# A router before a mixture-of-experts layer: logits the other way round, fewer table steps, later weight requests

## The reference, cut to what matters

```
tokens = layernorm(x).reshape(-1, 256)                 # 4096 tokens
probs  = softmax(tokens @ Wr + br)                     # 8 experts
expert = argmax(probs);  max_prob = probs[expert]
h   = relu(tokens @ W1[expert] + b1[expert])           # 256 -> 512
out = h @ W2[expert] + b2[expert]                      # 512 -> 256
x   = x + out * max_prob
```

## Time and profile before

| | us |
|---|---|
| median of 3 runs | 1510.41 |
| the profiled execution | 1510.09 |
| its span | 1508.1 |
| PE busy (x6834 matmuls) | 1358.1 (90%) |
| DVE / ACT / POOL busy | 1042.3 / 959.1 / 850.9 |
| chain that ended last | PE 63%, ACT 14%, DVE 13%, issue 8% |

### The profile page before, as it was taken

How to read it: one execution, slowest core, us unless ns; L and a number is a source line. 1 busy time by engine, 2 the same in 40 slices (tenths; PEclk the granted TensorE clock), 3 DMA queues, 4 the chain that set the end, 5 groups by cost and what they waited for, 6 DMA issues and landing times.

```text
span 1508.1 us, 21846 instructions
## 1 busy us (share of the span) xinstructions
PE 1358.1 (90%) x6834; PEld 922.1 (61%) x6834; DVE 1042.3 (69%) x1567; ACT 959.1 (64%) x1781; POOL 850.9 (56%) x413
## 2 busy tenths in 40 slices
PE   5999889999988988989989989999899878759997
PEld 2566645999744555555655655555556545449996
DVE  6666534333333898998899989998998998853332
ACT  1222231344325999898998998999989999104442
POOL 1111002555200898887888888878878889224552
PEclk9999999999988999999999999999999899979999
DMA  9200024676420697996996998979969989447662
GB/s 302 74 28 28 28 84 146 207 205 209 129 67 16 136 225 161 203 221 160 209 222 154 211 208 173 218 171 204 213 149 210 219 206 229 127 152 209 211 207 81
DMA packets 100116, 249.28 MB, mean 165 GB/s; under 512 B 10857, under 2 KB 41710, under 8 KB 85808
## 3 DMA queue, kind: packets, MB, share of 16 engines
q0 software_dynamic: 23248, 132.93, 40.6%
q1 hardware_dynamic: 74688, 113.62, 25.2%
q10 hardware_dynamic: 2080, 1.47, 0.3%
HBM read 116.65 MB, written 18.88 MB: 90 GB/s over the span
## 4 chain that ended last, share of the span: by engine, by line
PE 63%; ACT 14%; DVE 13%; issue 8%; DMA 1%; POOL 0%; DVEq 0%; POOLq 0%; ACTq 0%
PE ps L1515 11%; PE ps L1254 10%; PE ps L1455 9%; PE ps L1464 9%; ACT arena L698 5%; DVE arena L1152 5%; ACT arena L708 5%; PE ps L1546 4%; PE ps L1279 4%; PE ps L1316 2%; PE ps L1373 2%; PE ps L1270 2%; PE ps L1590 2%; PE ps L1411 1%; DVE x L1152 1%
## 5 line engine op out<-in xcount | busy, mean ns | idle before, releaser
L463 POOL TENSOR_TENSOR arena<-arena 128x2048 f32<-128x2048 f32 x97 | 446.4, 4602 | 149.7 <-DVE arena L1152 140.5
L1152 DVE TENSOR_TENSOR_SCAN arena<-arena,ps 128x512 f32<-128x512 f32 x392 | 471.4, 1212 | 60.6 <-PE ps L1254 52.2
L1254 PEld LDWEIGHTS ps<-cst,arena 128*128 128x128 f32 x2428 | 301.6, 145 | 322.4 <-issue 207.0
L1254 PE MATMUL ps<-cst,arena 128*128 128x128 f32 x2428 | 374.4, 282 | 79.0 <-ACT arena L708 39.2
L698 ACT ACTIVATE arena<-arena,a_neg 128x512 f32<-128x512 f32 x512 | 366.3, 715 | 46.1 <-DVE arena L1152 35.0
L708 ACT ACTIVATE arena<-arena,m_bt 128x512 f32<-128x512 f32 x512 | 363.2, 710 | 3.3 <-DVE arena L1083 2.2
L1515 PE MATMUL ps<-arena,tapw 128*128 128x512 f32 x512 | 260.5, 609 | 0.0
L432 POOL DMA_INDIRECT arena<-rows,arena x78 | 75.7, 970 | 176.9 <-DVE arena L1008 153.7
L1028 DVE TENSOR_TENSOR arena<-ps,arena 128x256 f32<-128x256 f32 x78 | 33.2, 426 | 202.9 <-PE ps L1464 120.3
L1152 DVE TENSOR_TENSOR_SCAN x<-arena,ps 128x512 f32<-128x512 f32 x120 | 143.9, 1211 | 19.9 <-PE ps L1254 17.0
L1455 PEld LDWEIGHTS ps<-arena 128*128 128x128 f32 x1248 | 153.5, 194 | 3.8
(11 more groups left out here) (168 smaller groups left out, 1552.3 us busy)
## 6 DMA issues: line engine op xcount, KB each, us to landing
arena<-arena POOLq DMA_DIRECT2D x52, 1024.0 KB, 8.3
arena<-in_W SPq DMA_DIRECT2D x94, 512.0 KB, 7.9
x<-arena POOLq DMA_DIRECT2D x33, 1024.0 KB, 8.3
arena<-c_rows SPq DMA_DIRECT2D x128, 256.0 KB, 3.7
arena<-x POOLq DMA_DIRECT2D x16, 1024.0 KB, 8.8
rows<-x SPq DMA_DIRECT2D x16, 512.0 KB, 3.4
x<-x POOLq DMA_DIRECT2D x8, 1024.0 KB, 9.1
x<-residual SPq DMA_DIRECT2D x12, 512.0 KB, 5.5
```

Source lines behind the costliest of these rows:

```text
L463: g.tensor_tensor(h, h, m_c[i % RC].unsqueeze(1).to_broadcast([P, KI, SEQ]), ALU.mult)\
L1152: v.tensor_tensor_scan(out=h[:, k, :], data0=m_a[g % RA], data1=ps[SCAN_BANK[g % 3]][:, :], initial=0.0, op0=ALU.mult, op1=ALU.add).then_i ...
L1254: return t.transpose(bank, src[:, k * P:(k + 1) * P], ident)
```

## The change

- `logits` takes the tokens as stationary operand (128 x 128) and the 8 router columns as moving, two matmuls per chunk and eight per batch, and writes 128 x 32 directly. `lg_copy` and `lg_turn` are gone. In round 0 `x_turn(0, 1)` comes ahead of `logits(0, 0)`.
- Rows in DRAM have 258 values: 256 of x, mean and rstd. ACT writes those two (`scales_out`): two DMAs of 8 bytes per token, in round 0 behind `raw_copy` of batch 5, in round 1 ahead of the exponential. The gathers wait for them. `r_val` has two values (token, max_prob) instead of four; `norm` reads mean and rstd from the gathered row.
- The counting matmuls change places: `ones` first, with its own semaphore step, then `tri`. DVE starts on the totals when `ones` is done. Rounding uses one constant of 2^30 size, so a tile number costs one step instead of three. 12 linked or unlinked steps are left of the 17.
- W1 of tile 1 and all later ones is asked for only when the first gather has landed.
- Taps: (0,0) goes ahead of the counting matmuls, (0,1) and (1,0) behind them, (1,1) behind the last group, and the last four behind the expert loop. The last conv load moves behind all W1 requests of round 0 on SP.

```
-FEED_PAIR = ([((0, 4), (5, 1), (2, 3))[i % 3] for i in range(BATCH)], ...
+FEED_PAIR = ([((0, 4), (5, 2), (1, 3))[i % 3] for i in range(BATCH)], ...
-ROUND = 1.5 * 2 ** 23
-V_TOK, V_PMAX, V_MEAN, V_RSTD, NV = 0, 1, 2, 3, 4
+CEIL = 1.5 * 2 ** 30
+V_TOK, V_PMAX, NV = 0, 1, 2
+ROW = D + 2
+RUN = NCH + 1
...
 # SP, send_w1 (the wait), and the taps' loads
                 for j in range(TILES):
+                    if j == 1:
+                        sp.wait_ge(S("f_x0"), 16 * (r * ((TILES + XB - 1) // XB) + 1))
...
+            for k in range(TAPS - 1):
+                send_tap(k)
             send_w1(0)
+            send_tap(TAPS - 1)
 # POOL, send_tiles
                 g.wait_ge(S(f"f{r}_rows"), 16 * BATCH)
+                g.wait_ge(S("scales_out"), 32 * (r + 1))
 # ACT
-            def lg_copy(r, i):
...
+            def scales_out(r):
+                half = RING * SEQ
+                a.wait_ge(S("f_scales"), r + 1)
+                for i in range(2):
+                    lo = half * (i ^ r)
+                    a.dma_start(xs[r][lo:lo + half, D:ROW].rearrange("(c p) v -> p c v", p=P),
+                                scales[:, i * NCH // 2:(i + 1) * NCH // 2, :]).then_inc(S("scales_out"), 16)
...
             def feed(r):
+                if r:
+                    scales_out(r)
 # DVE, feed
-                v.wait_ge(S("by_ones"), 2 * r + 2)
-                link(v.tensor_copy(tot, ps[6][:, 0:NCH * E].rearrange("p (c e) -> p e c", e=E)))
...
+                v.wait_ge(S("by_ones"), 3 * r + 2)
+                link(v.tensor_reduce(r_tl, total[:, :, 1:RUN], AX.X, ALU.add))
+                link(v.tensor_scalar(r_tl, r_tl, 0.5 * (P - 1), CEIL, ALU.add, ALU.add))
+                link(v.tensor_scalar(r_tl, r_tl, -CEIL, None, ALU.add))
                 link(v.tensor_tensor_scan(out=r_te, data0=ones[:, 0:E], data1=r_tl, initial=0.0,
                                           op0=ALU.mult, op1=ALU.add))
...
+                v.tensor_scalar(r_tc, r_te, CEIL, None, ALU.add)
+                link(v.scalar_tensor_tensor(out=total[:, :, 0], in0=r_te, scalar=-1.0, in1=r_tl, op0=ALU.add,
+                                            op1=ALU.subtract))
+                link(v.tensor_tensor_scan(out=r_cum, data0=cst[:, C_RST:C_RST + E * RUN], data1=ps[6][:, 0:E * RUN],
+                                          initial=0.0, op0=ALU.mult, op1=ALU.add))
+                v.wait_ge(S("by_ones"), 3 * r + 3)
+                link(v.tensor_tensor(pm, rank, cum[:, :, 0:NCH], ALU.add))
                 link(v.tensor_tensor(pm, pm, oh, ALU.mult))
+                link(v.tensor_reduce(r_pf, r_pm.rearrange("p (e c) -> p c e", e=E), AX.X, ALU.add))
...
+                link(v.tensor_scalar(r_hi, r_pf, -0.5 * (P - 1), CEIL, ALU.add, ALU.add))
+                v.scalar_tensor_tensor(out=r_pf, in0=r_hi, scalar=-CEIL, in1=r_pf, op0=ALU.add, op1=ALU.subtract)\
                     .then_inc(S("f_place"), 1)
 # PE
             def logits(r, i):
...
+                for c in range(CPB):
+                    for k in range(KD):
+                        last = t.matmul(ps[FEED_PAIR[r][i][0]][:, c * E:(c + 1) * E], x_turned[r][i][:, k, c * P:(c + 1) * P],
+                                        wr[:, k, :], start=(k == 0), stop=(k == KD - 1))
...
             x_turn(0, 0)
+            x_turn(0, 1)
             logits(0, 0)
-            lg_turn(0, 0)
+            t.wait_ge(S("f_xt"), 2)
             a_oturn(BATCH - 1, BATCH - 1)
-            x_turn(0, 1)
+            logits(0, 1)
             a_out(BATCH - 1)
...
             def feed(r):
+                if r == 0:
+                    t.wait_ge(S("f_raw"), BATCH - 1)
+                    tap(0, 0)
                 t.wait_ge(S("f_lg"), 2 * r + 2)
-                t.matmul(ps[5][:, 0:NCH * E], tri, r_oh, start=True, stop=True)
-                t.matmul(ps[6][:, 0:NCH * E], ones, r_oh, start=True, stop=True).then_inc(S("by_ones"), 1)
+                t.matmul(ps[6][:, 0:E * RUN].rearrange("p (e c) -> p e c", e=E)[:, :, 1:RUN], ones,
+                         r_oh.rearrange("p (e c) -> p e c", e=E), start=True, stop=True).then_inc(S("by_ones"), 1)
+                t.matmul(ps[5][:, 0:NCH * E], tri, r_oh, start=True, stop=True).then_inc(S("by_ones"), 1)
                 if r == 0:
-                    for n in range(3):
+                    for n in range(1, 3):
                         tap(n // KD, n % KD)
...
-                    if r == 0 and i == 0:
-                        tap(1, 1)
                 if r == 0:
-                    for d in range(KD):
-                        tap(2, d)
-                    t.wait_ge(S("tapw"), KD * 3)
+                    tap(1, 1)
+                    t.wait_ge(S("tapw"), KD * 2)
...
             feed(0)
-            for d in range(KD):
-                tap(TAPS - 1, d)
+            for n in range(4, KD * TAPS):
+                tap(n // KD, n % KD)
```

More of the change, by code:

```diff
@@ L95 @@
 FEED_ORDER = (tuple(range(BATCH)), (4, 5, 0, 1, 2, 3, 6, 7))
-FEED_PAIR = ([((0, 4), (5, 1), (2, 3))[i % 3] for i in range(BATCH)], [(0, 1)] * 6 + [(2, 3), (0, 1)])
+FEED_PAIR = ([((0, 4), (5, 2), (1, 3))[i % 3] for i in range(BATCH)], [(0, 1)] * 6 + [(2, 3), (0, 1)])
 FEED_AT = (2, 10, 18, 26, 34, 42)
@@ L128 @@
 C_RST = 4 * P
-C_THR = C_RST + E * NCH
-C_DESC = C_THR + NCH
+C_DESC = C_RST + E * RUN
 C_IOTA = C_DESC + E
@@ L153, in build @@
         vals = sb("vals", [P, NCH, NV])
-        mean, rstd, pmax = [vals[:, :, i] for i in (V_MEAN, V_RSTD, V_PMAX)]
+        scales = sb("scales", [P, NCH, 2])
+        mean, rstd, pmax = scales[:, :, 0], scales[:, :, 1], vals[:, :, V_PMAX]
         cst = sb("cst", [P, C_ALL])
@@ L240, in build @@
         s = Space(tail)
-        t_x = [s.take(D) for _ in range(XB)]
+        t_x = [s.take(ROW) for _ in range(XB)]
         t_n = [s.take(D) for _ in range(2)]
         t_xt = [s.take(KD * P).rearrange("p (k t) -> p k t", k=KD) for _ in range(2)]
-        assert s.at <= router + 4 * NCH * E, s.at
+        assert s.at <= router + 5 * NCH * E, s.at
         s = Space(AR - 2 * KI * DI - KI * D - 3 * HID)
@@ L274, in build @@
         x_turned = ([f_xt[i % 2] for i in range(BATCH)], [halves[i // IN_LAST][i % 2] for i in range(BATCH)])
-        lg_turned = ([f_flat[i % 2][0:E, 0:SEQ] for i in range(BATCH)],
-                     [late[i // IN_LAST][0:E, (i % 2) * SEQ:(i % 2 + 1) * SEQ] for i in range(BATCH)])
         lg_raw = (r_pm, m_bc[:, 0:NCH * E])
@@ L280, in build @@
         ps = [ctx.enter_context(nc.psum_tensor(f"ps{i}", [P, 512], F32)) for i in range(8)]
-        xs = [nc.dram_tensor(f"rows{r}", (TOK + 1, D), F32, kind="Internal").ap() for r in range(2)]
+        xs = [nc.dram_tensor(f"rows{r}", (TOK + 1, ROW), F32, kind="Internal").ap() for r in range(2)]
         c_rows = [nc.dram_tensor(f"c_rows{i}", (NS, SEQ), F32, kind="Internal").ap() for i in range(2)]
@@ L355, in _, with send_tap @@
             sp.dma_start(ipw, T["ip_x"].rearrange("(k p) d -> p k d", p=P)).then_inc(S("ld_cw0"), 16)
-            for k in range(TAPS):
+            def send_tap(k):
                 if k >= 2:
@@ L577, in _, with tap_copy @@
                         x_copy(0, i, k)
[L578 to L588 removed]
+                if i - 1 >= 2:
+                    raw_copy(0, i - 1)
+                if i == BATCH - 2:
+                    scales_out(0)
+            def tap_copy(n):
+                a.wait_ge(S("tap_mm"), n + 1)
+                a.activation(tapw[:, n // KD, n % KD, :], ps[n % 2][:, :], ACT.Copy).then_inc(S("tapw"), 1)
             def feed(r):
+                if r:
+                    scales_out(r)
                 a.wait_ge(S("f_lg"), 2 * r + 1)
@@ L593, in feed @@
                 if r == 0:
-                    for k in range(TAPS // 2):
-                        tap_copy(k)
+                    for n in range(3):
+                        tap_copy(n)
                     a.wait_ge(S("ld_m"), 16 * 9)
@@ L775, in _ @@
                     x_copy(1, i, k)
-                lg_copy(1, i)
                 raw_copy(1, i)
@@ L809, in layer_norm_scales @@
                 link(v.tensor_scalar(y.bitcast(I32), d.bitcast(I32), -0.5, 1597463007.0, ALU.mult, ALU.add))
-                for _ in range(3):
+                for i in range(3):
                     link(v.tensor_tensor(q, y, y, ALU.mult))
                     link(v.scalar_tensor_tensor(out=t, in0=q, scalar=-0.5, in1=d, op0=ALU.mult, op1=ALU.mult))
-                    link(v.scalar_tensor_tensor(out=y, in0=t, scalar=1.5, in1=y, op0=ALU.add, op1=ALU.mult))
+                    last = v.scalar_tensor_tensor(out=y, in0=t, scalar=1.5, in1=y, op0=ALU.add, op1=ALU.mult)
+                    if i == 2 and done:
+                        last.then_inc(S("f_scales"), 1)
+                        v.wait_ge(S("f_scales"), done)
+                    else:
+                        link(last)
             def ln_apply(out, c):
```

115 lines of the change are left out of this document (35 added, 80 removed).

## The result

The changed kernel takes **1502.09 us** (median of 19 runs, 1496.16 to 1510.02) against 1510.88 (median of 19, 1509.01 to 1514.68): ratio **0.9947, 95% interval 0.9936 to 0.9958**. It is faster, by 0.5% instead of the predicted 2.2%; 1477 us was missed by 25 us and the range (1469 to 1493) too. The runs of the new kernel spread over 14 us, those of the old one over 6. The profiled execution took 1499.49 us (span 1497.7; before: 1508.1).

What follows compares the result with a forecast made beforehand. The prediction took a chain of waits between engines in both routers as the bound. Savings of 21.6 (round 0), -0.5 (behind the loop), 1.2 (last mamba batch) and 10.7 (round 1) sum to 33.0: from 1510.09 to 1477 us, range 1469 to 1493.

Steps and rivals of the forecast that it cites:

- Logits, 7.7: Round 0's router logits: copy, turn back and copy go; six batches save 6.0, first and last 1.7, in all 7.7 us.
- the logits matmuls are therefore not cheaper: Round 0's logits: sixteen 8-column records per batch at 0.11 to 0.13 each take 1.8 to 2.1 us, against 1.83 before.
- rival B: Logits: eight moving columns leave PE nearly empty, clock halves from batch 2, 16 us lost, total 1493; chance 0.12.
- ScalarE's two issues, 0: Issue of the mean and rstd writes on ACT, 0.59 each (1.2 for two), taken to fit into slack and cost nothing.
- Totals and places, 2.8 in round 0: Between logits and groups: `ones` first with PE warm saves 1.3, fewer DVE steps for places save 1.5 us.
- Groups, 7.8 and 3.4: Four one-hot groups up to `idx`: shorter groups, fewer taps ahead in round 0; 7.8 us saved there, 3.4 in round 1.
- Gather to first tile, 3.3 and 4.0: From `idx` to first tile: gather lands 2.6 after its start, stretch falls to 6.0; saves 3.3 and 4.0 us by round.
- rival A: First tiles: the wait moves from the gather to late W1 weights, 4 us in each round, total 1485; chance 0.12.
- the term of zero: W1 of tile 1, asked for later: needed 4.1 us after its request, first in its queue, so no wait was priced.
- Rival C: The 8-byte writes hold the gathers: nothing at 30 ns each, 1488 at 81 ns; chances 0.06 without loss, 0.03 slower.
- Behind the loop, -0.5: After round 0's expert loop: four taps instead of two delay ACT's normalising; 0.5 us lost, bounds -0.5 to +1.7 lost.
- The last mamba batch, +1.2: Last mamba batch before round 1: six `lg_copy` leave ACT's chain; 1.2 us saved, bounds 0 to 2.8.

Runs made afterwards that it cites:

- combo2: Changed kernel with 128-column logits, 160-column one-hot products, six unread matmuls in round 1 and the scales' writes on SyncE: 1483.0 us.
- scales_sp: Changed kernel with the two writes of mean and rstd issued by SyncE instead of ScalarE: 1499.18 us, ratio 0.9930 to the kernel before.
- wide kernels: Variants of the changed kernel whose logits matmuls move the same 8 columns 16 times (128 columns); with that edit alone 1492.98 us, ratio 0.9884.
- wide_grp: Changed kernel with each one-hot product moving its 80 columns twice (160 columns): 1495.34 us, ratio 0.9902 to the kernel before.
- warm_grp: Changed kernel with 160-column one-hot products and, in round 1, six unread 512-column matmuls behind the two sums: 1494.11 us, ratio 0.9884.
- pitch: Changed kernel with 128-column logits and DRAM rows 1088 bytes apart instead of 1032, padding zeroed by two extra DMAs: 1510.29 us, ratio 0.9993.
- mixed: Changed kernel with 128-column logits in round 0 and the old kernel's logits in round 1: 1495.59 us, ratio 0.9903 to the kernel before.
- combo4: combo2 plus the edits of pitch and gate2; total slower than the expected 1475 to 1478 us, its own time not given in the text.
- combo6: combo2 with five unread matmuls instead of six and round 1's logits in the old form; slower than 1478 to 1480 us expected, last batch 75.1 us.
- gate2: Changed kernel with 128-column logits and W1's third and fourth slots asked for behind the first relu: 1499.19 us, ratio 0.9923.
- again: The changed kernel without any edit, profiled a second time: 1505.26 us, ratio 0.9947 to the kernel before.

## Why the prediction was wrong, step by step

The step that failed is one premise in two places: that PE does narrow products at full clock. It failed in round 0's logits and in round 1's groups.

**Logits, 7.7: the step that failed.** At full clock the term is right: copy, turn back and copy did go, and they were worth 7.84 (`combo2`), where the clock stays and ScalarE has no issue in its way, and a narrow batch took 2.61 against the forecast 2.7. The step "the logits matmuls are therefore not cheaper" priced sixteen records at full clock, and the clock did not stay: 3.2 in the first profile, a loss of 3.5 to 4.8 in four others, 6.1 in `scales_sp`. This was rival B, given 0.12. Its arithmetic doubled turn and logits from the third batch on, 16 us; measured are 4.6 to 12.5 above the forecast stretch in five profiles and 1.6 in `scales_sp`. So its term was too large, and its 1493 is too low all the same, since it kept all the other terms at full clock. I had set it aside by the earlier trace rows, where PE, 0.85 of 3.00 us busy with transposes alone, kept 1.00. That row shows a short stretch of light work at full clock; what had to be priced was 20 us of turns and 8-column products without a gap. No row of before showed that, so both ends should have stayed open. The same trace even had a row for the other side, in round 1's logits, behind some 15 us of turns with pauses between them (the same four records took 1.88 at full clock; mean clock 0.57 from 1225 to 1230):

```profile
1225.16 3.58 PE L1373 MATMUL ps<-arena,wr 128*8 128x512 f32 x4 [0.22 <-ACT arena L547]
```

The Trainium skill ("TensorE: Matmul & The Clock Gate", Part 4) says that transposes don't count as PE-busy the same way; the runs agree so far that turns with narrow products go cold and the same turns with wide products do not. PE's busy share says nothing here: it was 12.00 of 12.00 us at 0.50.

**ScalarE's two issues, 0: mis-sized.** 1.2 by the earlier trace rows, a row from the start, and taken as hidden; they took 2.57 and 5.44. In round 0 they cost 0.9 to 2.1 where the clock holds (wide kernels). In round 1 they turn 2.4 (totals and places) into 0.6; `scales_sp` gives 2.2 there.

**Totals and places, 2.8 in round 0: right at full clock,** 2.75; 2.0 in the first profile, with a tap that began cold (5.23 instead of 3.5).

**Groups, 7.8 and 3.4: the clock again.** Round 0 gave 6.4; the last group's 3.28 us cold is the rest, and where it is warm it is 7.7. Round 1 gave nothing (-0.2). The sum had "PE cold at first"; that it would then warm up, as in the kernel before, was assumed, and that kernel's products were twice as wide. `wide_grp` and `warm_grp` show it (14.4 and 12.4 instead of 16.5).

**Gather to first tile, 3.3 and 4.0: right in the main,** 2.4 and 3.7, and 3.4 where the tap beneath it is warm. In the changed kernel's own two profiles PE never waits for W1 of tile 1. In five variants it does, by 0.7 to 1.3 us in round 0 (`warm_grp` 1.13, `pitch` 1.27, `mixed` 1.19, `combo4` 0.70, `combo6` 0.93), and for the third tile's by 2.49 in `gate2`. So rival A, 4 per round, did not come, but the term of zero has little to spare. Not in the sum at all was the relu behind it: 2.3 us from first to second layer, and 1.5 more for the cold layer that follows.

**Rival C is false as told.** POOL never waits for the writes. Queue 10 went from 0.3% to 0.6% with 8256 packets more: 0.3% x 16 x 1498 / 8256 is about 9 ns each, its lower end. (Its break-even is also a little off: 256 writes of 130 ns are 33.3 us, 8.3 over the 25 of round 0 and 24.3 over the 9 left in round 1, 32.6 in all.) The writes cost at their issue instead.

**Behind the loop, -0.5: right** (-0.7, 8.7 to 8.0).

**The last mamba batch, +1.2: -3.2.** 1.5 goes with the narrow logits in the stretch ahead of it: from output product to output product 103.0 instead of 101.5, in all six narrow profiles (102.9 to 103.0), and 101.5 to 101.8 in all others. The other 1.7 are open. In the first profile DVE's wait for broadcasts is 2.6 longer, but in `again` it is 1.5 and POOL's 3.8, as in the kernel before, and the batch takes 72.1 all the same. The size changes with each kernel (70.1 to 78.2 us for a batch of 70.2 before), and neither pitch nor the logits' form explains it alone. This batch is also where `combo2` loses 6 of the 17 us that it had gained by then.

Put together for the profile: start -1.0 (the last attends lie that far apart, the execution's doing: those of the old kernel's own two profiles lie 2.9 apart), logits 3.2, totals and places 2.0, groups 6.4, gather 2.4, relu -2.3, cold first turns and loop -2.0, behind it -0.7, last batch -3.2, round 1 0.5 + 0.6 - 0.2 + 3.7 + 0.9: 10.3, and the spans differ by 10.4. Of the 33.0 forecast, 22.7 are missing here: 4.5 in the logits of round 0, 0.8 in totals and places, 1.4 in the groups, 0.9 at the gather, 4.3 behind it (relu and cold turns), 0.2 behind the loop, 4.4 in the last mamba batch, 5.2 in round 1 (3.6 of them the groups, 1.8 the scales' issue), and 1.0 at the start. So the logits are not the largest part in this profile. In `again`, with the same code, they miss the forecast stretch by 11.2.

## What to carry to other kernels

Removing copies between engines makes TensorE's own work denser but can make it lighter: price the step at both clocks unless a row shows this mix of work at 1.00, and if narrow products are bound by their weight loads, try them widened with repeated columns, which here cost 0.05 us a batch and held the clock. A DMA of many small pieces is priced by what waits behind its issue on that engine, and its issue is measured, not taken from another DMA's row. Gains ahead of a stage with many transfers came back smaller here (6 of 17 us lost in `combo2`), so read what such a stage does when it starts earlier.

## What was not expected of the hardware

- Full busy time at half clock: 8 moving columns behind 128x128 loads, 12.00 of 12.00 us busy, clock 0.50; with 128 columns 10.20 of 12.00 us, clock 1.00, and 0.05 us more per batch at full clock (2.66 against 2.61 us).
- The clock of one kernel falls at different points of the same code (in the products from 203.54 on in one profile, from 191.29 and, after a recovery, from 201.44 on in the other), which spreads one stretch by 6.6 us (34.0 to 40.6), and over all six narrow kernels by 10.9 (31.0 to 41.9).
- Two issues of 2048 8-byte pieces each took 1.30 to 8.70 us on the issuing engine.
- 57,344 zeros written in pieces of 56 bytes to each of two tensors at the start delayed the attention part by 11 us (`pitch`, and again `combo4`).
